# Two later batches follow the batch ahead by four steps of a wave instead of five

## The reference, cut to what matters

```
x = layernorm(x + L0_attn(x))     # attention, 8-step scan, feed-forward
x = layernorm(x + L0_ffn(x))      # one linear map (weight + a pooled low-rank part)
x = layernorm(x + L1_attn(x))     # attention without a mask
x = layernorm(x + L1_ffn(x))      # relu feed-forward

# inside L0_attn, after the causal attention:
x = x + attn
xs = ln(x, g1, b1); vs = 0; ctx = attn
for 8 steps:
    u  = tanh(ctx @ w_ctx + xs @ w_x + b_inl)
    vs = vs + 0.1 * (u - xs - vs)
    xs = xs + 0.1 * vs
x = x + xs
x = x + gelu(ln(x, g2, b2) @ ff_w1 + ff_b1) @ ff_w2 + ff_b2
```

## Time and profile before

| | us |
|---|---|
| three runs: lowest, median, highest | 1511.41, 1514.3, 1517.33 |
| the profiled execution | 1513.78 |
| its span, first to last instruction | 1512.0 |
| TensorE busy (share of the span) | 1366.1 (90%) |
| VectorE busy | 1251.6 (83%) |
| ScalarE busy | 1079.6 (71%) |
| GpSimd busy | 278.4 (18%) |
| mean granted clock of TensorE | 0.964 |

### The profile page before, as it was taken

One profiled execution on the slowest core, in us unless ns is written; L12 is line 12 of the kernel. 1 busy time (PEld: TensorE's weight loads), 2 busy tenths in 40 slices (PEclk: granted clock), 3 DMA queues, 4 the chain that ended last, 5 costly groups with the idle time before them and its releaser, 6 DMA issues.

```text
span 1512.0 us, 31977 instructions
## 1 busy us (share of the span) xinstructions
PE 1366.1 (90%) x13016; PEld 565.2 (37%) x13016; DVE 1251.6 (83%) x1715; ACT 1079.6 (71%) x1239; POOL 278.4 (18%) x624
## 2 busy tenths in 40 slices
PE   6699999999998768888679999999999999999886
PEld 3334434444443235456323332332333333323455
DVE  8988888888884386985899999999999999997043
ACT  6167777777777567763358888888888888888652
POOL 5022313222222151431100000000000000001252
PEclk9689999999999989999889999999999999999998
DMA  5510111101000000021110000000000000000001
GB/s 179 169 44 24 39 31 31 40 24 46 24 4 2 1 1 0 1 81 67 42 64 24 23 24 23 24 21 14 16 23 24 23 23 24 3 3 3 1 15 42
DMA packets 38995, 47.90 MB, mean 32 GB/s; under 512 B 11072, under 2 KB 20160, under 8 KB 38720
## 3 DMA queue, kind: packets, MB, share of 16 engines
q1 hardware_dynamic: 38416, 45.31, 9.8%
q10 hardware_dynamic: 432, 0.53, 0.1%
HBM read 30.22 MB, written 15.47 MB: 30 GB/s over the span
## 4 chain that ended last, share of the span: by engine, by line
PE 73%; DVE 11%; ACT 7%; issue 5%; POOL 3%; DMA 1%; ACTq 0%; POOLq 0%; SPq 0%; DVEq 0%
PE ps L428 29%; PE ps L406 15%; PE ps L385 12%; PE ps L554 7%; DVE l_negp L326 3%; PE ps L445 3%; ACT l_outT L304 2%; ACT shared L298 2%; POOL n_rs L516 2%; PE ps L391 2%; DVE n_bst L497 1%; PE ps L547 1%; PE ps L1042 1%; PE ps L910 1%; PE ps L562 1%
## 5 line engine op out<-in xcount | busy, mean ns | idle before, releaser
L326 DVE TENSOR_REDUCE l_negp<-ps 128x2 f32<-128x1024 f32 (+2 forms) x832 | 956.4, 1181 | 57.7 <-PE ps L391 33.3
L298 ACT ACTIVATE shared<-ps 128x1024 f32<-128x1024 f32 (+1 forms) x832 | 820.5, 991 | 185.3 <-PE ps L406 155.7
L428 PE MATMUL ps<-shared,l_vs 128*32 128x256 f32 (+3 forms) x6648 | 515.4, 385 | 18.9 <-ACT l_outT L304 14.1
L385 PE MATMUL ps<-Ks,Qs 48*128 48x512 bf16 (+3 forms) x1792 | 329.2, 368 | 31.1 <-DVE l_negp L326 22.0
L406 PE MATMUL ps<-Qs,Ks 51*128 51x512 bf16 (+3 forms) x1792 | 321.1, 367 | 14.5 <-ACT shared L298 6.3
L428 PEld LDWEIGHTS ps<-shared,l_vs 128*32 128x32 f32 x6648 | 136.6, 108 | 198.0 <-issue 163.4
L406 PEld LDWEIGHTS ps<-Qs,Ks 51*128 51x128 bf16 x1792 | 81.1, 93 | 316.8 <-issue 181.3
L385 PEld LDWEIGHTS ps<-Ks,Qs 48*128 48x128 bf16 x1792 | 87.5, 94 | 171.8 <-ACT shared L298 96.0
L282 POOL TENSOR_SCALAR_AFFINE_SELECT shared<-shared 128x512 f32<-128x512 f32 x128 | 81.7, 640 | 311.1 <-ACT shared L298 309.0
L267 POOL CAST l_parts<-l_negm 128x16 bf16<-128x16 f32 x64 | 12.6, 197 | 442.3 <-DVE l_negm L331 439.2
L391 PE MATMUL ps<-mask,id 64*128 64x128 bf16 x1024 | 68.5, 222 | 0.0
(11 more groups left out here) (160 smaller groups left out, 1094.7 us busy)
## 6 DMA issues: line engine op xcount, KB each, us to landing
Qs<-scr_q SPq DMA_DIRECT2D x128, 64.0 KB
Ks<-scr_k SPq DMA_DIRECT2D x64, 96.0 KB
Qs<-scr_q SPq DMA_DIRECT2D x128, 32.0 KB
Ks<-scr_k SPq DMA_DIRECT2D x64, 64.0 KB
scr_q<-own SPq DMA_DIRECT2D x4, 768.0 KB, 3.6
scr_q<-shared SPq DMA_DIRECT2D x4, 768.0 KB, 3.5
scr_k<-own SPq DMA_DIRECT2D x4, 768.0 KB, 4.9
scr_k<-shared SPq DMA_DIRECT2D x4, 768.0 KB, 4.8
```

Of the source, the lines that this page charges most:

```text
L298: act.activation(dst, src, ACT.Exp, scale=SCALE).then_inc(exped, 1)
L326: dve.tensor_reduce(dst, src, AX_X, ALU.max, negate=True).then_inc(reduced, 1)
L385: last = pe.matmul(outs[par], Qs[s][r:r + MROW, h2, qt * P:(qt + 1) * P], Ks[s][r:r + MROW, h2, at:at + w], start=True, stop=True)
L428: last = pe.matmul(pv_ps[32 * h:32 * h + 32, a:a + wide], vs[g % 2][:, kt, h, :], pT[m % PRING][:, h, a:a + wide], start=m == u.first_step ...
```

## The change

It changes two numbers of `MID_AT`. Batch 2 begins in wave 12 instead of 13, batch 3 in wave 16 instead of 18. Batch 3's v is then in wave 48, and what takes its place from `done` comes two waves earlier.

```diff
 RING = 3
 LEAD = 24
 PACE = 3
-MID_AT = (0, 8, 13, 18)
+MID_AT = (0, 8, 12, 16)
 LAST_AT = (0, 8, 10, 12)
```

## The result

The kernel got slower by a third of a per cent: 1520.57 us in the median of nine runs (1517.58 to 1523.32) against 1514.3 (1511.41 to 1521.15), ratio 1.0034 with a 95% interval of 1.0017 to 1.005, or some 5 us. The forecast was no change, 1514. The time lies in the range, and within the 0.5% in which, by the forecast, a measurement of this kernel can't tell a change from none; this one can, for the interval excludes 1.

A forecast was written before the change was run, and what follows sets the result against it. The stage was taken as bound by the order of its in-order queues. The steps +2.5 - 4.7 + 8.3 - 6.3 sum to -0.2, giving 1514 us against a median of 1514.3; range 1505.5 to 1521.

The forecast's parts named there:

- Turn4 to v of batch 1, +8.3: Waves 37 to 40 of the new order: 8.3 us longer, mainly from two more crossings; bounds +1.9 and +12.2.
- crossings: Wave boundaries where two maxima units share one bank pair, so TensorE waits for VectorE's queue; three forecast, one before.
- The three idle times: TensorE's waits for VectorE's reduction at the three crossings, forecast as 3.1, 1.55 and 4.8 us.
- V to q of batch 3, -6.3: Drain: two waves fall away (-10.7 us), 4.4 comes back; bounds -10.7 and -3.
- The three items that were to cost 4.4: Drain: batch 2's third parts (2.4 us) and add (1.2) on VectorE, and a turn4 at half clock (0.8).
- Up to batch 1's last scan, +2.5: Filling waves: earlier work of batches 2 and 3 delays this scan matmul by 2.5 us; bounds 0 and 5.
- From there to turn4, -4.7: Batch 1's last scan to its turn4: 94.2 us for 98.9; bounds -8.6 and -1.
- the term for TensorE's steps: Between batch 1's last scan and turn4: 29, 14 and 9 steps at full-clock start-to-start prices, 82.8 us for 80.1.
- From q of batch 3 to the first key: End of the stage: unchanged, 0, as the maxima keep their distance to the key.
- The first, that the waves simply fall away: Whole stage: waves keep their mean price, -8.7 us, so 1505.6; chance 0.24.
- The second: Drain: clock stays low behind the crossings, 8 us more, 1522; chance 0.19.
- The third, that the shifted batches wait for their banks: Shifted batches wait for banks or attention output, so the change moves nothing that counts, 1513.8; chance 0.02.

The follow-up runs named there:

- e3: Kernel before, batches unmoved, first six units of maxima two waves earlier, giving three crossings; 1523.64 us, ratio 1.0062 to the kernel before.
- e1: The changed kernel with its first maxima spread so that no crossings are left; 1508.38 us, ratio 0.9975 to the kernel before.
- e2: Kernel before with its first two maxima spread, so its one crossing goes; 1510.28 us, ratio 0.9968 to the kernel before.
- f1: Kernel before with batches 2 and 3 each one wave earlier (12 and 17), maxima spread, no crossings; 1508.38 us, ratio 0.994.
- g1: f1 plus matmuls nobody reads in TensorE's waits, by the table of f4; 1504.52 us, ratio 0.993 to the kernel before.
- f4: e1 plus matmuls nobody reads, put into five waits of TensorE; 1506.94 us, ratio 0.9942 to the kernel before.
- g3: The changed kernel, crossings kept, plus matmuls nobody reads by the table of f4; 1518.06 us, ratio 1.0019 to the kernel before.
- g2: f3 plus matmuls nobody reads in TensorE's waits, at places of its own; 1507.65 us, ratio 0.9961 to the kernel before.
- f3: Kernel before, batches unmoved, all 26 maxima ahead of the first key spread, no crossings; 1508.61 us, ratio 0.9959 to the kernel before.
- e4: Kernel before with only batch 3 one wave earlier (17), maxima as planned, two crossings; 1516.7 us, ratio 1.0021 to the kernel before.
- f2: Kernel before with only batch 3 one wave earlier (17), maxima spread, no crossings; 1508.71 us, ratio 0.996 to the kernel before.

## Why the prediction was wrong, step by step

**Turn4 to v of batch 1, +8.3: right, in mechanism and in size.** +9.1 in the change, and +8.5 in e3, where the same crossings stand on before's batches. The three idle times came within 0.31 us of what was worked out. By the runs, taking all three away gains 0.59% (e1), before's one is worth 0.32% (e2), two added cost 0.62% (e3). Taken together they put the two that the change adds between 4 and 9 us; 0.59% less 0.32% is the lower end, e3 the upper. The Trainium skill (Perfetto Trace Analysis, "Matmuls" under "Optimizing Tensor Performance") has the rule that independent matmul groups should rotate through PSUM banks; the runs agree in sign (two units back to back on one pair cost time in e3), and the price here is the consumer's whole queue, not one evacuation of 1.22.

**V to q of batch 3, -6.3: right.** -6.7, and nearly the same without crossings (e1 36.71). The three items that were to cost 4.4 stand in the changed kernel's trace: batch 2's two third parts at 748.84 and 750.04 on VectorE ahead of lin's statistics at 751.19, its add at 755.82 ahead of batch 3's scaling, and batch 3's turn4 at half clock (1.94).

**Up to batch 1's last scan, +2.5: wrong, +5.3.** Counted from batch 1's first transpose, batch 0's turn_xs came 1.7 later (predicted 1.5) and batch 1's third scan matmul 1.9 later. That the 1.7 agrees is partly luck: in the change the three steps ahead of turn_xs ran at half clock (1.94, 1.91 and 2.25 for 1.04, 1.04 and 1.88), and in f1, where the order up to there is the same, they ran at full clock and turn_xs stands at 30.02, for 30.32 before. Then the step failed at one sentence: "What is repaid is the wait at 568.28 ... and the matmuls behind it at half clock ... batch 1's fifth scan matmul is late by 1.2 alone." It is late by 3.95 (62.44 for 58.49); from there to the last scan it is 1.2 more, where 1.3 was predicted. The wait and the half clock were not repaid, they moved. TensorE of the kernel before in waves 15 to 17, ahead of the two lines in the earlier trace rows:

```profile
550.52 1.95 PE L554 MATMUL ps<-shared,wx 128*128 128x512 f32 x4 [1.57 <-DVE shared L826]
...
555.84 1.94 PE L547 MATMUL ps<-ident,own 128*128 128x128 f32 x8 [2.49 <-DVE own L535]
557.57 2.48 PE L554 MATMUL ps<-shared,wx 128*128 128x512 f32 x4
...
562.97 1.95 PE L554 MATMUL ps<-shared,wx 128*128 128x512 f32 x4 [1.20 <-DVE shared L826]
```

And of the changed kernel in the same waves, then behind two waits of the four-batch waves, for the earlier trace rows:

```profile
554.29 1.95 PE L554 MATMUL ps<-shared,wx 128*128 128x512 f32 x4 [2.41 <-DVE shared L826]
560.19 1.64 PE L547 MATMUL ps<-ident,own 128*128 128x128 f32 x8 [3.95 <-DVE own L535]
561.63 3.03 PE L554 MATMUL ps<-shared,wx 128*128 128x512 f32 x4
566.64 1.28 PE L547 MATMUL ps<-ident,shared 128*128 128x128 f32 x8 [1.98 <-DVE shared L535]
567.72 1.91 PE L547 MATMUL ps<-ident,attn_tm 128*128 128x128 f32 x8
569.43 2.55 PE L554 MATMUL ps<-own,w_sb 128*128 128x512 f32 x4
...
578.68 1.88 PE L554 MATMUL ps<-shared,wx 128*128 128x512 f32 x4
...
628.14 3.12 PE L554 MATMUL ps<-shared,wx 128*128 128x512 f32 x4 [2.32 <-DVE shared L826]
...
682.88 1.46 PE L547 MATMUL ps<-ident,shared 128*128 128x128 f32 x8 [2.79 <-DVE shared L535]
```

Before, TensorE waits 1.57, 2.49, 1.20 and 3.36 in these waves, 8.6 together; after, 2.41, 3.95 and 1.98, 8.3. The wait for batch 2's scaling shrank, and those for batch 1's update and batch 0's scaling grew, because batch 2's norm now stands ahead of them on VectorE. Half clock stayed too: against the durations at full clock (1.04 and 1.88) the rows of before hold some 3.3 us of it (1.94, 2.48, 1.27, 3.42) and those of after 3.5 (1.64, 3.03, 1.28, 1.91, 2.55). So the new steps found no cover: of the 5.3, 2.6 are twelve matmuls more (194 to 206: eight transposes and four of 512 columns), 0.9 clock, and 1.75 idle time (18.69 to 20.44).

f1, g1 and f4 take this apart. f1 has the same three waits (2.42, 3.96 and 1.99), yet counted from batch 0's turn_xs its fifth scan matmul of batch 1 is only 0.6 later than before (28.75 for 28.18); in the change it is 2.3 later (30.44). The change has batch 3's place beside the waits: from batch 2's turn1 at 566.64 to that scan matmul at 578.68 TensorE never waits, for 12.04 us. Among its steps there are batch 3's turn_attn and out, 2.59 at full clock, which the prediction lists nowhere ahead of this matmul; in f1, where out stands behind it, the same way takes 10.34. With TensorE kept busy the distance from turn_xs is 27.06 without out there (g1) and 28.76 with it (f4). So out costs 1.7 at either clock, and the half clock 1.7 in either order. The path there is TensorE's own queue; the prediction put the added steps in it at nothing and took the half clock as repaid.

In f4 the matmuls at 567.72 and 569.43 run at 1.04 and 1.88, and batch 1's fifth scan matmul is late by 2.0, not 3.95 (in g3 the same). So about 2 of the missing 2.75 are the clock, by experiment. VectorE's part of the step held: it gave batch 1's first two updates where the walk had them (550.9 and 557.9 less the 2.06 by which wave 8 is later; forecast 550.7 and 557.7), and the third a us later (564.4 for 563.4).

**From there to turn4, -4.7: wrong, -0.1.** The waits were listed well: 11.4 in the prediction, 10.26 measured (98.82 less 88.56), the three long ones 2.32, 1.71 and 2.79 where 2.6, 2.1 and 2.6 were forecast. What failed is the term for TensorE's steps: 82.8 at full clock, from start to start, and 88.56 measured. Of the 5.8 over, 3.4 are half clock: the steps behind the waits of 2.32 and 2.79 above take 5.21 for 3.44 and 4.33 for 2.66. The step took them at full clock because two longer waits, 3.12 and 3.59, had been followed by full clock. The other 2.3 have a counterpart before, 3.2 (83.33 busy less the 80.1): a step beside a wait takes more than the price from start to start (four matmuls 1.88 to 1.96 for 1.72, eight transposes 1.06 for 0.87). The prediction had these 3.2 among its 18.8 of "waits and clock" before and put nothing for them in the new order. f4 gets 2.2 back against e1; there the same wait of 2.32 was followed by full clock (1.96 at 623.99), and the one of 2.79 is filled. Before's own order in e2 took 99.60 for 98.91, so 0.7 is within what executions differ by.

**From q of batch 3 to the first key, "as before": wrong, +2.0.** The same 41 matmuls take 14.22 for 9.83, at a clock of 0.59 for 0.88. But this belongs neither to the shift nor to the crossings: e3, not shifted, has 19.69 at 0.76; e1, with no crossing, 20.76 at 0.75; and g2 and f3, in the same order there, 16.60 at 0.71 and 14.46 at 0.95. The clock is not all of it either, for g1 has 16.47 at 0.91. What decides that clock stays open; no bank pair is free there to keep TensorE busy.

**The sum.** The prediction let the waves pay for the crossings: -8.5 and +8.3. The crossings cost what they should, and the waves paid far less than that, which e1 against e2 shows without any crossing in play; f1 against f3 (0.994 and 0.9959, intervals that meet) leaves room for a gain from one wave, 0.19% or some 3 us if it is one. What two waves save in the drain (5.1 us between the traces of e1 and e2) the fill takes back (85.91 for 78.45 in these two), and the four-batch waves, which were to give 4.7, give nothing (99.77 for 99.60): partly by clock, partly by TensorE's own steps.

**The rivals.** The first, that the waves simply fall away, failed twice: the crossings are not hidden, and without them the saved waves still do not show. The second came near in time (1522) but not in place: between the crossings TensorE came back to full clock (k at 714.44 took 1.98), and the drain's clock is no better without crossings (0.75 in e1, 0.78 in the change). Half clock did cost more than was forecast, but ahead of the crossings (3.4 in the four-batch waves) and in the last stretch, where e1 has it too. The third, that the shifted batches wait for their banks, fails in the trace: batch 3's first transposes, at 567.72 above, have no wait of TensorE ahead of them. (The last output of the first attention, at 511.33, lies four waves ahead of batch 2's new place, not five; nothing hangs on it.) The Trainium skill (TensorE: Matmul & The Clock Gate, "What's actually happening") has activity as what releases the higher clock; f4's fill, at 0.96 where e1's is at 0.88 without the matmuls that nobody reads, agrees.

## What to carry to other kernels

Before work is moved earlier, count who still holds a buffer at the new place: a second unit on the same bank pair makes the producer wait for the consumer's whole queue (up to 4.49 us here for a reduction of 1.22), and one unit per wave takes that away. Fewer waves are not less time by the mean price of a wave where each wave is made of waits between in-order queues: a wait that a reordering "repays" must be followed to where it comes up next, with the clock behind it, and an earlier batch's own steps must be counted on every engine that they now stand on. Prices taken from start to start leave out what a step costs when a wait follows it. Here one unit per wave while a single pair is free, a lag of four for one batch alone, and matmuls in TensorE's longest waits gave 0.993 of the time before; the first of the three is shown by itself (f3, 0.9959), the other two add less than the runs resolve one by one.

## What was not expected of the hardware

Waits of TensorE as short as 2.32 and 2.79 us in a busy stretch were followed by matmuls at 1.2 GHz, though after 3.12 and 3.59 in the kernel before they ran at 2.4 GHz; and in f4 the very wait of 2.32, before the same matmul, was followed by 2.4 GHz (1.96 for 3.12). The length of the wait alone does not decide it.

Matmuls whose result nobody reads, put into such waits, raised the clock of the fill to 0.96 from 0.88. The kernels were shorter by 1.4 (f4), 3.9 (g1) and 2.5 us (g3) by the medians, each with intervals that meet those of the kernel without them; g2 gained nothing by the ratio, for later stretches ran slower instead.

Kernels with the same order up to a point reach it at different times: batch 0's turn_xs stands between 28.65 and 30.34 us behind batch 1's first transpose in the traces of before, e2, e3, e4, f2 and f3, whose order up to there is one. It is the clock of waves 12 and 13: the scan matmul at 538.33 in before takes 3.63, and the same one in f2, which has 28.65, takes 1.95.
